# Adding up the eight relations' self rows of a GNN's last dense stage on VectorE instead of GpSimd

## What is computed

```python
out = x @ W_self + b_self
for r in range(8):
    h = x @ W[r]
    # alpha: softmax over the node's edges of kind r and its self loop
    out = out + segment_sum(alpha[:, None] * h[src], dst) + bias[r]
x = _layernorm(x + out)
```

## Time and profile before

| what | value |
|---|---|
| median of 3 runs | 9338.36 us (9333.44 to 9340.42) |
| profiled execution, its own time | 9343.7 us |
| its span in the profile | 9341.9 us |
| PE busy | 4003.5 us, 43% |
| DVE busy | 3070.9 us, 33% |
| ACT busy | 752.9 us, 8% |
| POOL busy | 6093.2 us, 65% |
| PE clock granted over the span | 0.584 of full speed |

### The profile page before, as it was taken

One profiled execution on the slowest core, in us unless ns is written; L12 is line 12 of the kernel. 1 busy time (PEld: TensorE's weight loads), 2 busy tenths in 40 slices (PEclk: granted clock), 3 DMA queues, 4 the chain that ended last, 5 costly groups with the idle time before them and its releaser, 6 DMA issues.

```text
span 9341.9 us, 94657 instructions
## 1 busy us (share of the span) xinstructions
PE 4003.5 (43%) x17870; PEld 3357.5 (36%) x17871; DVE 3070.9 (33%) x5742; ACT 752.9 (8%) x2284; POOL 6093.2 (65%) x6325
## 2 busy tenths in 40 slices
PE   3333333353333333344333333345813454545478
PEld 2333333343333333333333333332413444444454
DVE  4222222243222222223111111114135555555654
ACT  0000000010000000000000000001101222212230
POOL 6777777735777777744777777750077777767603
PEclk7556555555555565655565555655555656656665
DMA  2111111112222222211111111111334444434410
GB/s 51 27 27 27 27 27 27 27 32 51 54 52 53 54 52 53 54 44 31 27 27 27 27 27 27 27 29 47 127 88 107 120 114 113 115 104 118 116 49 21
DMA packets 573312, 519.21 MB, mean 56 GB/s; under 512 B 355349, under 2 KB 355349, under 8 KB 573082
## 3 DMA queue, kind: packets, MB, share of 16 engines
q0 software_dynamic: 200704, 212.34, 12.3%
q1 hardware_dynamic: 343994, 245.79, 9.7%
q10 hardware_dynamic: 28384, 58.61, 1.7%
HBM read 414.69 MB, written 100.74 MB: 55 GB/s over the span
## 4 chain that ended last, share of the span: by engine, by line
POOL 50%; issue 23%; DVE 11%; PE 9%; DVEq 4%; DMA 2%; ACT 1%; POOLq 0%; ACTq 0%; SPq 0%; PEldq 0%
POOL gat L537 50%; DVEq L256 2%; PE p_a L855 2%; DVE oh L1072 2%; PE p_all L956 1%; PE p_all L763 1%; DVE sel L1282 1%; DVE sel L1286 1%; PE p_b L879 1%; PE p_a L809 0%; DVE sum_t L1305 0%; PE p_all L850 0%; PE p_b L950 0%; PE p_a L948 0%; DVE toh L1293 0%
## 5 line engine op out<-in xcount | busy, mean ns | idle before, releaser
L537 POOL DMA_INDIRECT gat<-x_d,idx x3136 | 2966.1, 946 | 1299.2 <-issue 1128.7
L757 PE MATMUL p_all<-oh,msg 128*66 128x128 f32 (+1 forms) x6272 | 1421.3, 420 | 2514.9 <-ACT msg L600 1276.5
L757 PEld LDWEIGHTS p_all<-oh,msg 128*66 128x66 f32 (+1 forms) x6272 | 1278.4, 228 | 2657.7 <-DVE oh L1072 2657.7
L537 POOL DMA_INDIRECT gat<-rel_d,idx x1568 | 1537.2, 980 | 1065.6 <-DMA idx<-key_d 593.2
L537 POOL DMA_INDIRECT gat<-in_x,idx x1568 | 1487.8, 949 | 497.2 <-issue 486.0
L757 PE MATMUL p_all<-oh,gat 128*64 128x128 f32 x3136 | 709.4, 419 | 1268.2 <-DMA gat<-x_d,idx 1268.2
L1072 DVE SCALAR_TENSOR_TENSOR oh<-dstf,fine_col,p_b 128x512 f32<-128x512 f32 x1578 | 1107.1, 743 | 441.1 <-issue 304.2
L757 PEld LDWEIGHTS p_all<-oh,gat 128*64 128x64 f32 x3136 | 638.3, 225 | 1339.0 <-issue 1339.0
L1084 DVE TENSOR_TENSOR sum_t<-sum_t,p_all 64x128 f32 (+1 forms) x588 | 164.8, 280 | 2726.7 <-PE p_all L757 2726.7
L879 PE MATMUL p_b<-oh,msg 128*72 128x128 f32 x3136 | 661.6, 399 | 74.7 <-DVE msg L1295 47.5
L871 PE MATMUL p_all<-trip_s,oht 128*128 x1616 | 139.0, 237 | 1168.4 <-DVE oht L1278 1168.0
(11 more groups left out here) (241 smaller groups left out, 3536.3 us busy)
## 6 DMA issues: line engine op xcount, KB each, us to landing
he_d<-gat ACTq DMA_DIRECT2D x196, 288.0 KB
ea<-he_d SPq DMA_DIRECT2D x196, 288.0 KB
ea<-in_edge_attr SPq DMA_DIRECT2D x196, 256.0 KB, 2.6
gat<-x_d,idx POOLq DMA_INDIRECT x3136
drow<-dst_d SPq DMA_DIRECT2D x196, 256.0 KB, 3.7
rel_d<-sum_t SPq DMA_DIRECT2D x14, 2016.0 KB, 6.7
gat<-in_x,idx POOLq DMA_INDIRECT x1568
gat<-rel_d,idx POOLq DMA_INDIRECT x1568
```

The costliest lines, as they stand in the source:

```text
L537: nc.gpsimd.indirect_dma_start(out=gat[:, q, s, 0:width], out_offset=None, in_=table, in_offset=bass.IndirectOffsetOnAxis(ap=idx[:, q, s:s ...
L757: ins = nc.tensor.matmul(p_sum[0:width, 0, 0:W], lhs(q, s), oh[:, 0, s, :], start=(s == 0), stop=(s == S - 1))
```

## The change

GpSimd's loop in the last stage goes, with the semaphores `s_self`, `s_selfsum` and `s_pch`. Step 0 of `finish5` on VectorE gets a reduction in front of its addition: it reads `self_h` of a block, 7 x 8 x 64 elements in each partition, with the relation as the innermost dimension, so that successive elements read lie 64 elements (256 bytes) apart, and writes 7 x 64 sums to `yb`. `yb` is scratch of the same layer norm and is written again in step 3. The relations are added up in another order than by the tree.

```diff
-        s_self, s_selfsum = sem("s_self"), sem("s_selfsum")
-        s_vch, s_pch = sem("s_vch"), sem("s_pch")
+        s_vch = sem("s_vch")
@@ gpsimd
             gather_pass(3, rel_d, HROW)
-
-            with pool.Fori(0, NI) as it:
-                for u in range(2):
-                    wait_reg(pool, s_self, it * 2 + (u + 1))
-                    width = R * D // 2
-                    v = self_h[u].rearrange("p t r d -> p t (r d)")
-                    for step in range(3):
-                        nc.gpsimd.tensor_tensor(v[:, :, 0:width], v[:, :, 0:width], v[:, :, width:2 * width], ALU.add)\
-                            .then_inc(s_pch, 1)
-                        wait_reg(pool, s_pch, it * 6 + (u * 3 + step + 1))
-                        width //= 2
-                    pool.sem_inc(s_selfsum, 1)
@@ vector, scale_self
                 for k in range(2):
                     m = (BT * u + BT - 1 - (BT * u + BT - 1 + k) % 2) // 2
                     wait_reg(dve, s_hc[1][k], it * BT + (m + 2))
-                dve.sem_inc(s_self, 1)
@@ vector, finish5
                 if step == 0:
-                    wait_reg(dve, s_selfsum, b + 1)
-                    ch(vec.tensor_tensor(ya[:, :, :], self_y[u], self_h[u][:, :, 0, :], ALU.add))
+                    ch(vec.tensor_reduce(out=yb[:, :, :], in_=self_h[u].rearrange("p t r d -> p t d r"), op=ALU.add,
+                                         axis=AX.X))
+                    ch(vec.tensor_tensor(ya[:, :, :], self_y[u], yb[:, :, :], ALU.add))
```

## The result

The changed kernel takes 9407.38 us (median of 4 runs, 9404.35 to 9409.31), the kernel before 9338.74 (4 runs, 9333.44 to 9340.42). The ratio is 1.0074, with a 95% interval of 1.0057 to 1.0092: 0.74% slower. 9409 was forecast.

The account below looks back on a forecast made before the run. The last stage was taken as bound by TensorE and VectorE's evictions, GpSimd's sums hidden; 13 blocks at 5.57 us late, 72.4 us, less 1.8 at the end, gave +70.6 and 9409 us, range 9373 to 9432.

Parts of the forecast that it names:

- What bounds the stage: Last stage: TensorE and VectorE's evictions set the beat; GpSimd's some 100 us of sums are hidden except after the last block.
- R: Time of the new reduction on VectorE at step 0: 6.13 us, at 1.67 ns per element plus 0.14 us.
- The rival of a free step: Reduction at step 0 runs at the contiguous rate, 3.90 us; whole kernel 9378 us; chance 17%.
- The dear rival: Reduction on 128 partitions costs 2.04 ns per element, 7.45 us; whole kernel 9427 us; chance 11%.
- 7.58 us from eviction 0 to eviction 1: VectorE, a block's first two PSUM tile evictions: starts 7.58 us apart with the reduction between, in place of 1.69.
- What TensorE gets back: After its stall for eviction 1, TensorE recovers 0.32 us by eviction 3: 3.10 us in place of 3.42.
- 5.57 a block: Each of 13 blocks is 5.57 us late from eviction 3 on (5.89 less 0.32), 72.4 us in all.
- the ring passes through VectorE's step 4 as well as through TensorE: Block's end: TensorE's next turn of rows also needs ScalarE's copy, queued behind VectorE's step 4; TensorE idles 0.80 us for it.
- The end: Behind the last block: 7.14 us from L1546 to L1531 in place of 8.96, a gain of 1.8 us.
- The sum: Whole kernel: 72.4 less 1.8 gives +70.6 us, 9409 us against the median, 0.76% slower.
- The clock: TensorE's clock stays at 0.50; rival: it goes up in the idle gaps, 9345 us, not slower; chance 4%.
- The idle 7 us would hold R entirely: VectorE's idle 7 us before `self_w` could hold the reduction, but it stands behind the next block's first eviction.

Follow-up runs that it names:

- e3: Changed kernel with the reduction reading neighbouring elements in one buffer's blocks and elements 8 apart in the other's (wrong sums); last stage 355.3 us against 368.8.
- e9: Changed kernel with the reduction done a second time ahead of step 4, result unused; last stage 447.8 us against 368.8.
- e8: Changed kernel with ScalarE's copies of block b+2 put ahead of its root of block b; last stage 368.8 us, as in the changed kernel.
- e6: Changed kernel with the tree's three sums on VectorE behind a block's last eviction, replacing the reduction; last stage 294.2 us against 298.3 before the change.
- e1: Changed kernel with the reduction moved from step 0 to right behind a block's last eviction; last stage 299.3 us against 298.3 before the change.

## Why the prediction was right, step by step

- **What bounds the stage**: right. Taking GpSimd's 100 us of additions away gave nothing but the end.
- **R**: 6.13 forecast, 6.18 measured. The one row of 512 elements on one partition, with the same operation and the same step, told the price on 128. The rival of a free step (3.90) is a true price, 3.88 in e3, but for steps of up to 8 bytes; so the rule of the Trainium skill that the prediction set beside it, one element per cycle whatever the strides, did not hold for the step of 256 bytes. The dear rival (7.45, from a copy) didn't come.
- **7.58 us from eviction 0 to eviction 1**: 7.62 and 7.68 in the two kinds of block.
- **What TensorE gets back**: 0.32 forecast from the one row of 3.10. In the changed kernel, where TensorE really waits, evictions 1 and 3 are 3.01 to 3.03 apart (9253.77 to 9256.78), so 0.40. In the earlier trace rows the eviction at 9319.08 stood on TensorE's own beat (three tiles of 1.70 behind 9313.98, where the block began), so 3.10 was only an upper bound, and the reading of it as TensorE's way back was wrong. That it lay only 0.08 off is luck. TensorE's idle time is 5.2 us, where some 5.5 were forecast.
- **5.57 a block**: 5.53 and 5.6. The two small misses, 0.07 and 0.08, cancel.
- **"So the ring passes through VectorE's step 4 as well as through TensorE"**: this step was wrong as it stood. ScalarE's copies had 0.3 to 0.9 us of slack (e9), and moving them did nothing (e8). It didn't harm the sum, since both ends were late by the same 5.57; with an instruction at step 4 it would have mis-sized the sum by up to 0.9 a block, as the 451 expected of e9 against 447.8 shows.
- **The end**: a gain of 1.8 forecast, 1.76 measured.
- **The sum**: +70.6 us forecast, +70.5 in the stage. The median moved by 68.6, within the scatter of the gather passes.
- **The clock**: 0.50 on the whole stretch from 9060 to 9390 us; TensorE's 5 us gaps did not change it.
- **"The idle 7 us would hold R entirely"**: nearly. It holds the 3.8 us of the three sums (e6), and misses narrowly with 6.2 (e1, 1.0 us over the kernel before).

## What to carry to other kernels

Price an instruction by what stands behind it in its engine's program until the next place where that engine waits, not by the engine's busy share: the same 6.2 us cost 5.6 a block ahead of evictions that TensorE waits for, 5.3 to 5.95 ahead of the step that ScalarE waits for, and nothing behind both. In an engine with idle time of its own, move the work to the wait that holds that time. And one instruction in place of three is no gain where it has to jump: find a row with the same step before trusting the rate of a contiguous one.

## What the runs showed of the hardware

- VectorE's reduction in fp32 reads 3584 elements in 3.88 us with steps of 4 or 8 bytes and in 6.12 to 6.55 us with steps of 16 to 256 bytes. That 16 and 32 bytes would be the dearest I had not forecast; why they are is open.
- On one chip the same program took about 11930 us and on another about 9340, with the last stage of the same length. The time lies in the gather passes: the idle time ahead of GpSimd's gathers of `x` was 2436 us in e1 against 1298 in the changed kernel, while one gather took 951 against 944 ns; over all three kinds of gather the idle time was 5416 against 2860 us, which is 2556 of the 2589 by which the last stage began later. The cause wasn't looked for.
